# Four graph layers on one core: the input loads move from SyncE's queue to ScalarE's, and every engine's list is drawn anew

## The reference

```python
h = relu(layernorm(x)); x = x + L0(h)   # deg * (h Wi + b) + adj @ (h Wj)
h = relu(layernorm(x)); x = x + L1(h)   # softmax(mask(leaky(e_src[i] + e_dst[j]))) @ (h W)
h = relu(layernorm(x)); x = x + L2(h)   # the same with 128 columns; its output is [attn @ hW, hW]
h = relu(layernorm(x)); x = x + L3(h)   # 8-head attention with a mask, and an output projection
```

## Time and profile before

| | us |
|---|---|
| median of 3 runs | 1279.04 (1275.73 to 1283.11) |
| the profiled execution's own time | 1272.41 |
| its span, first to last instruction | 1270.4 |
| PE busy | 1219.8 (96%) |
| ACT busy | 1089.3 (86%) |
| DVE busy | 1081.4 (85%) |
| POOL busy | 1063.1 (84%) |

### The profile page before, as it was taken

How to read it: one execution, slowest core, us unless ns; L and a number is a source line. 1 busy time by engine, 2 the same in 40 slices (tenths; PEclk the granted TensorE clock), 3 DMA queues, 4 the chain that set the end, 5 groups by cost and what they waited for, 6 DMA issues and landing times. The chain is left out here.

```text
span 1270.4 us, 43726 instructions
## 1 busy us (share of the span) xinstructions
PE 1219.8 (96%) x12001; PEld 1112.8 (88%) x12001; DVE 1081.4 (85%) x5141; ACT 1089.3 (86%) x3975; POOL 1063.1 (84%) x1848
## 2 busy tenths in 40 slices
PE   7799999999999999999999999999999999999996
PEld 5589998998999988988988889898889989889986
DVE  5799998997999898898988888888889988888874
ACT  3579998997999888898988888888989988889996
POOL 4789888987889888888888889888889888888764
PEclk8999999999999999999999999999999999999999
DMA  6323333433343353432424433434333433431001
GB/s 164 63 51 53 59 67 66 57 70 67 56 70 67 56 68 69 56 73 64 56 70 67 56 61 67 66 62 57 70 64 63 67 65 68 63 52 30 19 19 35
DMA packets 97678, 78.57 MB, mean 62 GB/s; under 512 B 31648, under 2 KB 89248, under 8 KB 97440
## 3 DMA queue, kind: packets, MB, share of 16 engines
q1 hardware_dynamic: 94960, 74.07, 33.4%
q10 hardware_dynamic: 2480, 1.71, 0.5%
HBM read 58.79 MB, written 16.95 MB: 60 GB/s over the span
## 5 line engine op out<-in xcount | busy, mean ns | idle before, releaser
L886 ACT ACTIVATE exps<-masked,nmax 128x128 f32<-128x128 f32 x1024 | 396.9, 393 | 0.0
L418 POOL TENSOR_TENSOR probs<-exps,rsum 128x512 f32<-128x512 f32 x256 | 266.0, 1041 | 2.8 <-DVE rsum L660 2.8
L652 DVE CUSTOM_DVE_ANT_0 masked<-bank,mask 128x128 f32<-128x128 f32 x1024 | 230.3, 287 | 2.4 <-PE bank L1111 2.3
L389 POOL TENSOR_SCALAR y<-x,nm,rstd 128x256 f32<-128x256 f32 x384 | 210.7, 556 | 23.1 <-issue 21.7
L538 DVE BATCH_NORM_STATS2 stats<-x 128x6 f32<-128x256 f32 x512 | 189.1, 412 | 15.5 <-DMA x<-in_x 11.0
L886 ACT ACTIVATION_READ_ACCUMULATOR exps<-masked,nmax 128x1 f32 x1024 | 197.5, 193 | 0.0
L994 PE MATMUL bank<-w_hi,ht_hi 128*128 128x512 f32 (+1 forms) x512 | 186.7, 365 | 3.1 <-DVE ht_lo L599 1.6
L366 POOL TENSOR_TENSOR rstd<-veps,power 128x2 f32<-128x2 f32 x256 | 182.3, 712 | 0.1
L995 PE MATMUL bank<-w_lo,ht_hi 128*128 128x512 f32 (+1 forms) x512 | 175.5, 343 | 0.0
L996 PE MATMUL bank<-w_hi,ht_lo 128*128 128x512 f32 (+1 forms) x512 | 175.3, 342 | 0.0
L1119 PE MATMUL bank<-ident,probs 128*128 128x128 f32 x1024 | 143.3, 273 | 2.9 <-DVE t L568 0.6
(11 more groups left out here) (130 smaller groups left out, 3975.4 us busy)
## 6 DMA issues: line engine op xcount, KB each, us to landing
x<-in_x SPq DMA_DIRECT2D x64, 256.0 KB, 4.7
xt_sb<-in_xt SPq DMA_DIRECT2D x64, 256.0 KB, 5.7
out<-x SPq DMA_DIRECT2D x64, 256.0 KB
db<-rows SPq DMA_DIRECT2D x110, 128.0 KB, 4.2
mean_b<-rows SPq DMA_DIRECT2D x62, 128.0 KB, 3.3
rows<-dst SPq DMA_DIRECT2D x110, 1.0 KB, 4.8
rows<-mv SPq DMA_DIRECT2D x62, 1.0 KB
probs<-in_w0t ACTq DMA_DIRECT2D x1, 256.0 KB, 6.3
```

The lines of the kernel that those rows point to most:

```text
L389: last = pool.tensor_scalar(y[i][:, b, g], src[:, bx, g], nm[i][:, s, g:g + 1], rstd[i][:, s, g:g + 1], ALU.add, ALU.mult)
L418: pool.tensor_tensor(probs3[:, p % BUFFERS["probs3"], j], exps3[:, p % BUFFERS["exps3"], j], rsum3[:, s, j].unsqueeze(2).to_broadcast([P, ...
L652: last = dve.tensor_tensor_reduce(masked3[:, b, j, i], bank_of(f"sc{j}")[:, i * P:(i + 1) * P], mask[:], scale=-1.0, scalar=-MASKED, op0=A ...
L886: last = act.activation(exps3[:, b, j, i], masked3[:, p % BUFFERS["masked3"], j, i], ACT.Exp, bias=nmax3[:, s, j, i:i + 1], scale=-1.0, ac ...
```

## The change

ACT now issues the two loads of every pair from the third on; SP keeps the rows and the stores. LAG, BANKS and the order of every engine's list are new. The kernel's mathematics, tiles and buffers are as before. The core of the diff, with two lines of the tables:

```diff
-       "row_out1": 11, "row_in1": 11, "load": 6, "store": 18, "row_out0": 7, "row_in0": 7, "row_out2": 12,
+       "row_in1": -2, "row_in0": -5, "row_out2": -1, "store": 4, "row_out0": -6, "row_in2": -1,
...
-    "hh": (6, "hh_mm", ('hh',)),
+    "hh": (3, "hh_mm", ('hh',)),
...
         @block.sync
         def _(sp):
-            def load(p):
-                b = p % BUFFERS["x0"]
-                read_before(sp, "x0", p, "stats0", "r0")
-                sp.dma_start(x0[:, b], x_pairs[bass.ds(p, 1)].rearrange("o n g d -> (o n) g d")).then_inc(x_in[b], 16)
-
-            def load_transposed(p):
-                b = p % BUFFERS["xt"]
-                read_before(sp, "xt", p, "h0r")
-                sp.dma_start(xt_sb[:, b], xt[bass.ds(p, 1)].rearrange("o p c g n -> (o p) c g n")).then_inc(xt_in[b], 16)
...
             def step(t):
-                if due(t, "loadt") and t - LAG["loadt"] >= 2:
-                    load_transposed(t - LAG["loadt"])
-                if due(t, "row_in2") and not at_an_end(t - LAG["row_in2"]):
-                    spread_row(2, t - LAG["row_in2"])
                 if due(t, "row_out1") and not at_an_end(t - LAG["row_out1"]):
                     write_row(1, t - LAG["row_out1"])
                 if due(t, "row_in1") and not at_an_end(t - LAG["row_in1"]):
                     spread_row(1, t - LAG["row_in1"])
-                if due(t, "load") and t - LAG["load"] >= 2:
-                    load(t - LAG["load"])
+                if due(t, "row_in0") and t - LAG["row_in0"] >= MEANS_BY_TRANSPOSE:
+                    spread_means(t - LAG["row_in0"])
+                if due(t, "row_out2") and not at_an_end(t - LAG["row_out2"]):
+                    write_row(2, t - LAG["row_out2"])
                 if due(t, "store"):
                     store(t - LAG["store"])
                 if due(t, "row_out0") and t - LAG["row_out0"] >= MEANS_BY_TRANSPOSE:
                     write_means(t - LAG["row_out0"])
-                if due(t, "row_in0") and t - LAG["row_in0"] >= MEANS_BY_TRANSPOSE:
-                    spread_means(t - LAG["row_in0"])
-                if due(t, "row_out2") and not at_an_end(t - LAG["row_out2"]):
-                    write_row(2, t - LAG["row_out2"])
+                if due(t, "row_in2") and not at_an_end(t - LAG["row_in2"]):
+                    spread_row(2, t - LAG["row_in2"])
...
         @block.scalar
+            def load(p):
+                b = p % BUFFERS["x0"]
+                read_before(act, "x0", p, "stats0", "r0")
+                act.dma_start(x0[:, b], x_pairs[bass.ds(p, 1)].rearrange("o n g d -> (o n) g d")).then_inc(x_in[b], 16)
```

More of the change, by code:

```diff
@@ L47 @@
     "prepa": (0, "adj_spread", ('adj_rows',)),
[L48 to L51, removed]
-    "hh": (6, "hh_mm", ('hh',)),
[L53 to L57, removed]
     "ot": (3, "ot_mm", ('ot_lo',)),
-    "h0t": (0, "h0t", ('d0s',)),
+    "h0t": (4, "h0t", ('d0s',)),
+    "at1": (0, "e1t", ('at1',)),
     "v": (6, "v_mm", ('v',)),
-    "at1": (0, "e1t", ('at1',)),
-    "wh0": (4, "wh0_mm", ('wh0',)),
     "wh1": (5, "wh1_mm", ('wh1',)),
     "x2b": (0, "x2_mm", ('x2',)),
-    "pt2": (4, "pt2", ('p3t_2',)),
+    "wh0": (4, "wh0_mm", ('wh0',)),
+    "pt1": (1, "pt1", ('p3t_1',)),
     "x1b": (3, "s0", ('x1',)),
     "h3t": (5, "h3t", ('h3t_lo',)),
[L68 to L73, removed]
-    "kt": (5, "kt_mm", ('kt',)),
[L75 to L78, removed]
+    "pt2": (4, "pt2", ('p3t_2',)),
+    "x4b": (1, "x4_mm", ('x4',)),
+    "prep": (5, "products", ('w1_split',)),
+    "d2": (6, "d2", ('z2',)),
+    "m1": (0, "m1", ('mj_lo1', 't0_1')),
+    "m0": (2, "m0", ('mj_lo0', 't0_0')),
+    "kt": (5, "kt_mm", ('kt',)),
+    "qt": (1, "qt_mm", ('qt',)),
+    "at2": (4, "e2t", ('at2',)),
+    "h2t": (3, "h2t", ('ht2',)),
+    "pt0": (6, "pt0", ('p3t_0',)),
+    "d1": (5, "d1", ('z1',)),
+    "pt3": (0, "pt3", ('p3t_3',)),
+    "x3b": (4, "x3_mm", ('x3',)),
+    "hh": (3, "hh_mm", ('hh',)),
+    "h1t": (6, "h1t", ('h1t_lo',)),
+    "sc0": (1, "scores", ('nmax3_0',)),
+    "sc1": (5, "scores", ('nmax3_1',)),
+    "sc2": (2, "scores", ('nmax3_2',)),
+    "sc3": (4, "scores", ('nmax3_3',)),
     "h0r": (7, "h0r", ('h0t_lo',)),
     "zz2": (7, "z2", ('nmax2',)),
+    "zz1": (7, "z1", ('nmax1',)),
 }
@@ L473, in step @@
                     normalise(3, x3, t - LAG["y3"])
+                if due(t, "p3_0"):
+                    normalise_p3(0, t - LAG["p3_0"])
+                if due(t, "degr"):
+                    scaled_degree(t - LAG["degr"])
                 if due(t, "rsum1"):
@@ L680, in step @@
                     prepare_rows()
+                if due(t, "d0s") and t - LAG["d0s"] < MEANS_BY_TRANSPOSE:
+                    subtract_first_means(t - LAG["d0s"])
+                if t == LAG["w1_split"]:
+                    split_w1()
+                if due(t, "rsum3_0"):
+                    inverse_sum3(0, t - LAG["rsum3_0"])
+                if due(t, "mj_lo1"):
+                    low_mj(1, t - LAG["mj_lo1"])
+                if due(t, "mv0") and t > LAG["mv0"]:
+                    mean_and_variance(0, t - LAG["mv0"])
@@ new lines, in step @@
+                if due(t, "mj_lo0"):
+                    low_mj(0, t - LAG["mj_lo0"])
+                if due(t, "t0_0"):
+                    add_own(0, t - LAG["t0_0"])
+                if due(t, "x3"):
+                    sum_x3(t - LAG["x3"])
+                if due(t, "nmax1"):
+                    mask_logits(1, mask, t - LAG["nmax1"])
+                if t == LAG["w0_low"]:
+                    low_w0()
+                if due(t, "stats3"):
+                    stats_of(3, x3, t - LAG["stats3"])
@@ L925, in step @@
+                if due(t, "wh1"):
+                    copy_projection1(1, t - LAG["wh1"])
                 if due(t, "wh0"):
                     copy_projection1(0, t - LAG["wh0"])
-                if due(t, "wh1"):
-                    copy_projection1(1, t - LAG["wh1"])
-                if due(t, "exp3_1"):
-                    exps3_of(1, t - LAG["exp3_1"])
+                if due(t, "p3t_1"):
+                    copy_p3_transposed(1, t - LAG["p3t_1"])
                 if due(t, "v"):
                     copy_v(t - LAG["v"])
+                if due(t, "load") and t - LAG["load"] >= 2:
+                    load(t - LAG["load"])
@@ new lines, in step @@
+                if due(t, "h3t_hi"):
+                    relu_transposed_high(3, ht3_r, last_of("kt_mm", "qt_mm", "v_mm"), t - LAG["h3t_hi"])
+                if t == LAG["w3_high"]:
+                    round_w3()
+                if t == LAG["w0_high"]:
+                    round_w0()
+                if due(t, "loadt") and t - LAG["loadt"] >= 2:
+                    load_transposed(t - LAG["loadt"])
+                if due(t, "exp3_0"):
+                    exps3_of(0, t - LAG["exp3_0"])
+                if due(t, "z2"):
+                    sum_logits(2, hh, "hh", F1, t - LAG["z2"])
@@ L1200, in step @@
                     transpose_y(2, t - LAG["h2t"])
+                if due(t, "pt0"):
+                    transpose_p3(0, t - LAG["pt0"])
+                if due(t, "d1") and at_an_end(t - LAG["d1"]):
+                    spread_dst(1, wh, "wh", last_of("wh0", "wh1"), D + 1, t - LAG["d1"])
+                if due(t, "pt3"):
+                    transpose_p3(3, t - LAG["pt3"])
+                if due(t, "x3_mm"):
+                    attend(2, hh, "hh", F1, t - LAG["x3_mm"])
+                if due(t, "hh_mm"):
+                    project2(t - LAG["hh_mm"])
+                if due(t, "h1t"):
+                    transpose_y(1, t - LAG["h1t"])
+                if due(t, "scores"):
+                    scores(t - LAG["scores"])
             idle_products(14)
```

238 lines of the change are left out of this document (98 added, 140 removed), and 24 rows, old and new, of the table LAG.

## The result

In the same job the changed kernel took 1288.9 us (median of 5 runs, 1286.6 to 1291.2) and the kernel before 1279.7 us (5 runs, 1275.7 to 1283.1). The ratio is 1.0075, with an interval of 1.0048 to 1.0102: 0.75% slower, where 1247 us had been predicted, with a range of 1236 to 1277.

What follows compares the result with a forecast made beforehand. PE was taken as the bound at 18.41 us a pair, with 36.8 us lost to late rows queued on SP. 1272.4 - 36.8 + 11.2 left for row 1 = 1246.8, so 1247 us; range 1236 to 1277.

Steps and rivals of the forecast that it cites:

- Banks and lists: PE's unchanged products and new bank waits: no gain under 18.41 us a pair; `ot` has 1.0 us spare, cost nothing.
- the remainder of row 1: Loss left from row 1's late landings: 0.2 us a pair, 11.2 us in all, bounds 0 and 36.8.
- Row 2's path: Row 2's `dst` write on SP no longer queues 4.5 us behind the means' read; its stalls all go.
- Row 1's path: Row 1's write and read on SP, with narrower time: 1.1 us spare before ACT waits; 0.2 us a pair taken.
- the floor: PE's busy time for a pair, 18.41 us, the least a pair takes while the products stay the same.
- The row of the means: The means' read on SP goes out later, landing at 180.7, before POOL needs it: cost nothing, 1.9 us cover.
- The two loads on ACT: Loads of x and `xt` issued by ACT, beside its arithmetic: cost taken as nothing, at most 0.81 us a pair.
- the upper bound of 0.81 us: Both load issues on ACT if uncovered, 0.385 + 0.42 us a pair, still less than ACT's 1.27 us idle.
- The slow rival: ACT sets the pace through slow load issues, slower above 1.93 us of issue a pair: 1316 us, chance 0.12.
- The first sign named as "Wrong": Pairs of one constant length above 18.41 us, PE waiting at the same task in each, for a bank or ACT.

Runs made afterwards that it cites:

- the order alone: The kernel before with SP's rows in the new order and lags, both loads still issued by SP: 1242.5 us, ratio 0.9196.
- either end cut: The changed kernel with one instruction moved back early: `rsum3_3` on DVE (1235.7 us) or `rsum1` on POOL (1236.2 us).
- the new queues alone: The kernel before with the loads issued by ACT and SP's new list and lags, other lists unchanged: 1249.1 us, ratio 0.9860.
- the trip put in: The kernel before, queues unchanged, with `rsum1` right ahead of `p3_3` on POOL and `rsum3_3` behind `stats2` on DVE: 1352.4 us, ratio 1.0004.

## Why the prediction was wrong

**The step that failed** is "Banks and lists": "Of the new bank waits I looked at the one of `ot` ... Cost: nothing". It looked at one wait of PE; the new orders on DVE and POOL stand in no term of the sum. The runs put 56 x (19.36 - 18.41) = 53.2 us in place of that nothing: the round trip between POOL and DVE. With it and with the remainder of row 1 at zero the sum is 1272.4 - 36.8 + 53.2 = 1288.8 us; the profiled execution took 1288.84. As 19.36 is measured, this says only that start and end stayed as they were. That the two moved instructions carry it is shown from both sides: with either one back it goes, and put into a kernel that keeps all lists but SP's it comes.

It could have been read off. The new order has DVE's `x2`, `stats2`, `rsum3_3` in a row between POOL's `rsum1` and `p3_3`; by the rows of before these take 0.87 + 0.75 + 0.16 = 1.8 us. From one `dst2` to the next (164.25 to 182.67) POOL had 18.42 - 0.67 - 0.31 = 17.4 us of work of its own. About 1 us was free, and 1.8 were asked for. (Over the 56 pairs POOL was busy for 928.8 of 1067.7 us, 87%, DVE for 88% and ACT for 89%, not for over nine tenths as said ahead of the prediction.)

**Row 2's path** went as predicted: the wait for `db` fell from 82.5 to 3.8 us, that for the means' landing from 344.7 to 17.7. The run with the order alone shows that this is SP's order. In the changed kernel the longer pairs could hide late rows, but not in the kernels without the trip: with either end cut, or both, and the loads on ACT, ACT has no wait for `db` at all, in pairs of 18.38 us.

**Row 1's path** was put at 0.2 us a pair, 11.2 in all. In the kernels without the trip it costs nothing that can be seen: 18.38 us a pair, which is even 0.03 under the 18.41 that the prediction called the floor. So the change without the trip reaches the low end of the range (1236 us).

**The row of the means** cost nothing, as predicted: POOL waited for it once, for 1.0 us.

**The two loads on ACT** cost nothing in the steady state of the changed kernel, as predicted. Their issues on ACT (ns: shortest, median, longest; first and last start in us):

```profile
L798 ACTq DMA_DIRECT2D x<-in_x x62: 374/374/375, 9.7 to 1122.4; - x62
L803 ACTq DMA_DIRECT2D xt_sb<-in_xt x62: 347/362/1929, 13.4 to 1142.8; - x62
```

The reason given, that ACT's issuing part works beside its arithmetic, holds for what stands ahead of an issue, not for what stands behind it. Nor does the upper bound of 0.81 us for both issues of a pair hold: `xt` alone took up to 1.93 us here and 2.93 in the run of the new queues alone, where eight long issues cost 9.5 us. In the changed kernel ACT had time to spare; in the kernels with an end cut, or both, no issue in the 53 pairs took over 1.35 us, and the pairs show none of it. That the start is some us shorter with the loads on ACT was not foreseen (the prediction allowed 5.3 either way for one landing).

**The rivals.** The slow rival had the sign and the wrong engine: the issues stayed far below its 1.93 us a pair. Its mechanism, ACT held up by a long issue, is there in the run of the new queues alone, at 9.5 us in all instead of 80.6. The rule quoted with it (the Trainium skill, Perfetto Trace Analysis, "DMA Instruction — HWDGE (DVE, Sync)") is that an issue waits for the lock of the shared block while another sequencer uses it. It is not the whole account of the long issues of `xt`: the one of 1.93 us in the changed kernel goes on for 1.56 us after the only issue of SP beside it has ended. In the run of the new queues alone each of the eight ends within 0.03 us of an issue of SP, but the longest had already lasted 1.79 us when SP's issues beside it began. What these issues waited for stays open. A rival "two lists wait for each other" was missing. The first sign named as "Wrong", pairs of one constant length, was the one that came, though PE waited neither for a bank nor for ACT:

```profile
PEld bank L1010 <- issue: 23.5, 53, 0.5
PEld bank L1010 <- POOL y L381: 18.7, 60, 1.2
```

The longest idle times of PE's loads are ahead of the transposes of `y`, which POOL makes, the engine that was late.

## What to carry to other kernels

When lists are drawn anew, take every pair of engines that hand work to each other and look for a hand-over that comes back: A waits for B at one place of its list, and B's list has, ahead of what A wants, something that waits for A's work just ahead of that place. Its length less what A has to do in between is idle time of A in every turn, and what counts is whether A can spare it. In this case turns of one constant length above the busiest engine's work were the sign of such a trip, and turns that spread that of late transfers or long issues.

## What was not expected of the hardware

The kernel that depends on its transfers is also the one that depends on the job: the kernel before took 1265 to 1350 us in four jobs. Of the others two were run in two jobs each: the changed kernel took 1288.9 and 1292.7 us, the one with an end cut and the loads back on SP 1241.9 (in the job of 1350) and 1239.2. In the job of 1350 us the median landings of row write and row read, seen in the kernel with the trip put in, were 5.1 and 4.5 us, against 4.8 and 4.2 in the earlier trace rows: 0.3 us each. The kernel before itself was not traced there, so that these 0.3 us made the difference is argued and not shown.
